# Scores in front of transposes, and odd heads' minima in front of the low half, in a four-layer attention kernel

## The reference

```python
def _L1_xattn_ref(text_hidden, vision_tokens, vision_mask, Wq, Wk, Wv, Wo):
    q = (text_hidden @ Wq).reshape(B, T_text, 16, 128).transpose(0, 2, 1, 3)
    k = (vision_tokens @ Wk).reshape(B, T_vis, 8, 128).transpose(0, 2, 1, 3)
    v = (vision_tokens @ Wv).reshape(B, T_vis, 8, 128).transpose(0, 2, 1, 3)
    k, v = jnp.repeat(k, 2, axis=1), jnp.repeat(v, 2, axis=1)
    scores = jnp.einsum('bhtd,bhsd->bhts', q, k) / scale
    attn = jax.nn.softmax(jnp.where(mask, scores, -jnp.inf), axis=-1)
    out = jnp.einsum('bhts,bhsd->bhtd', attn, v)
    return out.transpose(0, 2, 1, 3).reshape(B, T_text, 2048) @ Wo
...
x = x + _L0_xattn_ref(_layernorm(x), fside, ctx)
x = x + _L0_ffn_ref(_layernorm(x), w1, w2, w3)
x = x + _L1_xattn_ref(_layernorm(x), ctx, mask, Wq, Wk, Wv, Wo)
x = x + _L1_ffn_ref(_layernorm(x), router, sh_gate, sh_up, sh_down, r_gate, r_up, r_down)
```

## Time and profile before

| what | value |
|---|---|
| median of 3 runs | 386.31 us (386.14 to 386.44) |
| the profiled execution | 386.44 us, of which 384.7 us are the span from the first to the last instruction |
| TensorE matmuls | 373.3 us busy, 97% of the span |
| TensorE weight loads | 351.8 us, 91% |
| VectorE | 299.6 us, 78% |
| ScalarE | 233.9 us, 61% |
| GpSimd | 162.2 us, 42% |
| mean granted TensorE clock | 0.998 of full speed |

### The profile page before, as it was taken

How to read it: one execution, slowest core, us unless ns; L and a number is a source line. 1 busy time by engine, 2 the same in 40 slices (tenths; PEclk the granted TensorE clock), 3 DMA queues, 4 the chain that set the end, 5 groups by cost and what they waited for, 6 DMA issues and landing times.

```text
span 384.7 us, 8390 instructions
## 1 busy us (share of the span) xinstructions
PE 373.3 (97%) x2966; PEld 351.8 (91%) x2966; DVE 299.6 (78%) x982; ACT 233.9 (61%) x616; POOL 162.2 (42%) x260
## 2 busy tenths in 40 slices
PE   6899999999999999999999999999999999999996
PEld 6798789999798999999999999999999999999896
DVE  4798889889967889888767999887768876765644
ACT  1798787867544466766554466766554676664332
POOL 2113876874633344344453345246343333332232
PEclk9999999999999999999999999999999999999999
DMA  7999210000000200000000200000000000000000
GB/s 248 337 373 398 71 32 2 2 2 0 3 2 0 82 5 3 2 1 3 0 29 2 60 1 2 0 3 3 1 29 2 0 3 0 3 0 2 29 2 27
DMA packets 15193, 16.93 MB, mean 44 GB/s; under 512 B 1584, under 2 KB 14128, under 8 KB 15152
## 3 DMA queue, kind: packets, MB, share of 16 engines
q1 hardware_dynamic: 15152, 16.40, 12.7%
HBM read 15.34 MB, written 1.05 MB: 43 GB/s over the span
## 4 chain that ended last, share of the span: by engine, by line
PE 76%; DVE 12%; ACT 5%; POOL 3%; issue 2%; DMA 1%; DVEq 0%; SPq 0%; POOLq 0%
PE bank_qa L405 11%; PE bank_u L640 7%; PE bank_o L659 7%; PE bank_pt L624 7%; PE bank_s L604 6%; PE bank_s L405 5%; PE bank_o L663 4%; PE bank_u L644 3%; PE bank_s L612 3%; PE bank_s L522 3%; PE bank_pt L405 3%; PE bank_u L744 2%; PE bank_x L414 2%; PE bank_pt L522 1%; ACT prob L1010 1%
## 5 line engine op out<-in xcount | busy, mean ns | idle before, releaser
L1314 POOL TENSOR_SCALAR prob<-prob,row_inv,valid_b 128x256 f32<-128x256 f32 x128 | 70.3, 559 | 84.0 <-DVE row_inv L1684 84.0
L1010 ACT ACTIVATE prob<-prob,row_min 128x256 f32<-128x256 f32 x128 | 64.1, 503 | 40.9 <-DVE row_min L1676 40.8
L1689 DVE TENSOR_TENSOR pt_lo<-bank_pt,pt_hi 128x512 fp32r<-128x512 f32 x64 | 43.9, 686 | 14.8 <-ACT pt_hi L963 14.8
L1676 DVE CUSTOM_DVE_ANT_0 prob<-bank_s,masked 128x256 f32<-128x256 f32 x128 | 48.5, 417 | 0.9 <-ACT masked L992 0.6
L1325 POOL TENSOR_TENSOR act_lo<-act_raw,act_hi 128x256 fp32r<-128x256 f32 x32 | 24.1, 754 | 44.3 <-ACT act_hi L1077 44.2
L963 ACT ACTIVATE pt_hi<-bank_pt 128x512 fp32r<-128x512 f32 x64 | 37.6, 587 | 4.0 <-PE bank_pt L624 3.7
L624 PE MATMUL bank_pt<-ident,prob 128*128 128x128 f32 x256 | 39.5, 275 | 0.5 <-POOL prob L1314 0.3
L604 PE MATMUL bank_s<-cxT_hi,qa_hi 128*128 128x256 f32 x128 | 38.0, 319 | 0.0
L405 PE MATMUL bank_qa<-xt_hi,a_hi 128*128 128x256 f32 x126 | 35.0, 278 | 0.0
L405 PE MATMUL bank_qa<-xt_lo,a_hi 128*128 128x256 f32 x126 | 35.0, 278 | 0.0
L405 PE MATMUL bank_qa<-xt_hi,a_lo 128*128 128x256 f32 x126 | 35.0, 278 | 0.0
(11 more groups left out here) (325 smaller groups left out, 1190.2 us busy)
## 6 DMA issues: line engine op xcount, KB each, us to landing
wq_raw<-in_wqT SPq DMA_DIRECT2D x4, 512.0 KB, 8.7
wo_raw<-in_wo SPq DMA_DIRECT2D x4, 512.0 KB, 7.7
w_raw<-in_w12T SPq DMA_DIRECT2D x2, 704.0 KB, 7.1
gate_raw<-in_gateT SPq DMA_DIRECT2D x2, 576.0 KB, 7.3
up_raw<-in_upT SPq DMA_DIRECT2D x2, 576.0 KB, 9.0
down_raw<-in_downT SPq DMA_DIRECT2D x2, 576.0 KB, 10.8
x<-in_x SPq DMA_DIRECT2D x4, 256.0 KB, 5.9
guT<-in_guT SPq DMA_DIRECT2D x4, 256.0 KB, 3.6
```

What stands on the lines that cost most here:

```text
L1010: act.activation(row, row, ACT.Exp, scale=-1.0, bias=row_min[:, h % 2, t:t + 1], accum_out=row_sum[:, h % 2, t:t + 1]).then_inc(S["s_exp"], 1)
L1314: pool.tensor_scalar(row, row, row_inv[:, h % 2, t:t + 1], valid_b[:, 0:1], ALU.mult, ALU.mult).then_inc(S["s_norm"], 1)
L1676: dve.tensor_tensor_reduce(out=prob[:, h % 2, t, :], in0=src[:, t * T:(t + 1) * T], in1=masked[:, :], scale=1.0, scalar=3.0e38, op0=ALU.ad ...
L1689: dve.tensor_tensor(pt_lo[:, :, cols], bank["pt"][:, :].rearrange("p (s t) -> p s t", s=2), f32(pt_hi[:, :, cols]), ALU.subtract).then_inc ...
```

## The change

In TensorE's attention loop the scores of head h+2 are sent in front of the transposes of head h instead of behind them. In VectorE's loop the minima of head h+2 are taken in front of the low half of head h when h is odd, and behind it, as before, when h is even. Since the minima write over `prob` of head h, which the transposes read, the odd ones get a wait of their own for the transposes (`t_mm`); before, the low half's wait for `pt_hi` stood for that.

```diff
             def attention(b, beside=None):
 
                 for h in range(H):
-                    turn_probs(b, h)
                     if h + 2 < H:
                         scores(b, h + 2)
+                    turn_probs(b, h)
                     if h + 4 < H:
                         queries(b, h + 4)
...
                         row_inverses(b, h + 1)
                     if h >= 1 and h - 1 == mix_heads(mix_unit(h - 1))[-1]:
                         mix_lo(b, mix_unit(h - 1))
+                    if h % 2 == 1 and h + 2 < H:
+                        dve.wait_ge(S["t_mm"], H * b + h + 1)
+                        row_minima(b, h + 2)
                     probs_lo(b, h)
-                    if h + 2 < H:
+                    if h % 2 == 0 and h + 2 < H:
                         row_minima(b, h + 2)
```

## The result

The changed kernel takes **392.79 us** (392.68 to 392.95, 4 runs), the kernel before 386.23 us (386.06 to 386.44, 4 runs) beside it: a ratio of 1.0168, interval 1.0155 to 1.0180, or +6.6 us. The forecast was 391.0, in a range of 386.4 to 394.5. The profiled execution's span went from 384.7 to 391.1 us. All times here are medians; one execution of the kernel with the scores in front at odd heads took 740.11 us and is left out of its median.

What follows compares the result with a forecast made beforehand. TensorE was taken as the bound, without gaps inside the pairs. Losses at M's low-half waits summed to 4.9 us, less 0.2 for transposes: +4.7 on 386.44, 391.1, forecast as 391.0 us, range 386.4 to 394.5.

Steps and rivals of the forecast that it cites:

- TensorE sets the end and a new order can win only its few waits: Inside the 28 attention pairs: TensorE has no gaps; transposes wait at most 0.5 us in the run, 0.2 taken as gain.
- The tightest wait is M's for the low half: M's wait for the low half of a pair's second head has least slack: 0.36 to 1.19 us by place.
- The later transposes and the earlier minima add up at the odd low half: At the odd head's low half: 0.7 us from each, less VectorE's idle time there, 0.32 or nothing.
- first rival: Only one of the two delays counts, the later T being swallowed: about 386.7 us, no change; chance 0.08.
- second: Rival: minima fill VectorE's wait for `pt_hi`, so not slower: 385.9 us, or down to 384.2; chance 0.09.
- The undisturbed pair keeps 0.28: Batch 3, heads 6 and 7: odd low half 0.91 us late against 1.19 slack, no wait, 0.28 to spare.
- The rival with VectorE as the bound throughout: Four other pairs of batches 0 to 2 wait 0.4 us too, +4.8: 396 us; chance 0.08.
- The fourth pair loses 0.6: Heads 6 and 7, batches 0 to 2: low half 1.4 us late against 0.8, TensorE waits 0.6, three times.
- First and second pairs lose 1.1 and 0.9: First pairs: 0.4 us each in batches 1 and 2, 0.3 in batch 0; second pairs of batches 0 to 2: 0.3 each.
- The start of batch 3 loses 0.7: S(2) waits for `qa_lo`, delaying T(0); odd low half 1.24 us late against 0.53, 0.7 lost.
- The seventh pair loses 0.1, four times: Heads 12 and 13, each batch: low half about 0.8 us late against 0.8, 0 to 0.2 lost, 0.1 taken.
- the wait for `t_mm` costs nothing: Odd heads on VectorE: minima come after the inverses of head h+1, which end later than T(h), so no cost.

Runs made afterwards that it cites:

- the later transposes alone: Scores in front of transposes on TensorE, VectorE's order as in the kernel before: 392.48 us against 386.57, ratio 1.0151.
- the minima alone: VectorE's new order of minima only, TensorE's order as in the kernel before: 388.24 us against 386.57, ratio 1.0039.
- three heads, 0.6 us here: Kernel before with scores in front only at heads 1 and 3 of batch 0 and head 1 of batch 3: 385.93 us against 386.50, ratio 0.9985.

## Why the prediction was right, and what in it was off

- *TensorE sets the end and a new order can win only its few waits.* Right. The transposes' waits went (L624's idle time 0.5 to 0.0). The fifth pairs gained 0.24: in batch 1 two of T(8)'s transposes started 0.16 us behind the one ahead, while GpSimd finished, and now follow at 0.11. The third pairs gained 0.20, of which I know no cause.
- *The tightest wait is M's for the low half.* Not so, and the kernel before shows it. Its seventh pair in batch 1:

```profile
182.69 0.60 ACT L963 ACTIVATE pt_hi<-bank_pt 128x512 fp32r<-128x512 f32 x1 [0.56 <-PE bank_pt L624]
183.32 0.69 DVE L1689 TENSOR_TENSOR pt_lo<-bank_pt,pt_hi 128x512 fp32r<-128x512 f32 x1 [1.00 <-ACT pt_hi L963]
...
183.89 0.40 PE L640 MATMUL bank_u<-pt_hi,cx_hi 128*128 128x512 f32 x1
...
184.82 0.62 PE L644 MATMUL bank_u<-pt_lo,cx_hi 128*128 128x512 f32 x2
```

The low half ends at 184.01, 0.81 us ahead of L644; the high half ends at 183.29, only 0.60 ahead of L640. It is so in most pairs: 0.64 against 0.80 in the fourth, 0.32 against 0.53 at the start of batch 3, 0.05 against 0.36 in the first pairs of batches 1 and 2 (where the prediction saw it and still counted the low half). Only in the second pairs of batches 0 to 2 was the low half the tighter, by 0.04.

- *The later transposes and the earlier minima add up at the odd low half.* Right at the fourth pair, where either half alone costs 0.24 or 0.06 and both 0.76, and at the second (0.02 and 0.03 against 1.04 in all). Not true of the run as a whole: of +6.6 us the later transposes alone make +5.9, the minima alone +1.7, since without the minima in front other things are late. The first rival, under which the later T is swallowed and the time stays, is out by the +5.9; the second, under which VectorE hides it all, by the result.
- *The undisturbed pair keeps 0.28.* Measured 0.31, and no loss in the five middle pairs of batch 3. The rival with VectorE as the bound throughout is out: the third, fifth and sixth pairs of batches 0 to 2, which it had waiting, lose nothing.
- *The fourth pair loses 0.6.* It loses 0.76. The wait itself was 0.42 at the low half; the term lacked 0.11 us of restart behind each of two waits and the small wait of 0.05 at the high half, which makes 0.69.
- *First and second pairs lose 1.1 and 0.9.* Measured 1.33 and 1.04. The second pairs lose it at the low half. In the first pairs M is 0.73 late for the low half and 1.31 for the high half by the starts, and some of that is won back ahead of M.
- *The start of batch 3 loses 0.7.* Measured 1.06, and undoing that head brings 0.92 of it back. The rows:

```profile
308.65 0.68 DVE L1657 TENSOR_TENSOR qa_lo<-bank_qa,qa_hi 128x512 fp32r<-128x512 f32 x1
...
309.39 0.50 PE L612 MATMUL bank_s<-cxT_hi,qa_lo 128*128 128x256 f32 x2 [0.32 <-DVE qa_lo L1657]
...
311.74 0.66 PE L624 MATMUL bank_pt<-ident,prob 128*128 128x128 f32 x4
...
313.06 0.57 ACT L963 ACTIVATE pt_hi<-bank_pt 128x512 fp32r<-128x512 f32 x1
...
313.69 0.51 PE L640 MATMUL bank_u<-pt_hi,cx_hi 128*128 128x512 f32 x1 [0.59 <-ACT pt_hi L963]
```

S(2) waits for `qa_lo` as forecast, but the wait is handed on to the high half of head 1: M starts only when `pt_hi` ends at 313.63, while the low half behind it costs little more (0.16). The term looked at the low half alone.

- *The seventh pair loses 0.1, four times.* **This is the step that failed**: it loses 1.58 in all. I sized it by the low half, with a slack of 0.8; what is late is again M's high half, whose slack was 0.60. Batch 1, heads 12 and 13:

```profile
185.93 0.60 PE L624 MATMUL bank_pt<-ident,prob 128*128 128x128 f32 x4
...
186.56 0.60 ACT L963 ACTIVATE pt_hi<-bank_pt 128x512 fp32r<-128x512 f32 x1 [0.91 <-PE bank_pt L624]
...
186.83 0.40 PE L663 MATMUL bank_o<-c_hi,ut_lo 128*128 128x256 f32 x2
...
187.21 0.51 PE L640 MATMUL bank_u<-pt_hi,cx_hi 128*128 128x512 f32 x1
...
187.56 0.40 PE L640 MATMUL bank_u<-pt_hi,cx_lo 128*128 128x512 f32 x1
```

`pt_hi` follows its transposes at once and ends at 187.16, 1.23 us after they start. The two L663 matmuls stand 0.12 apart, so M would start at 187.06: with S in front, 1.13 us of matmuls are left between T(13) and M, where with S's 0.7 behind T(13) there were 1.83 and 0.60 to spare. M starts 0.15 late and its second matmul another 0.11, which makes 1.04 of the 1.58 over four batches. With the scores alone in front the seventh pairs lose no less (1.82), so it does not hang on the minima. That the wait for `t_mm` costs nothing was reasoned wrongly here too: T(13) ends after the inverses of head 14, and at each head 13 VectorE waits for it. It cost no time: the low half was still 0.16 us or more ahead of L644.

```profile
DVE prob L1676 <- PE bank_pt L624: 2.7, 4, 0.9
```

The losing terms came to 4.9 us and measured 7.3; the gains of the other places, 0.6, bring the sum to 6.7 (6.4 in the span, where the tail gives 0.3 back). The difference of 2.4 lies within the 2.8 that the prediction gave its 14 waits, but not wait by wait: the start of batch 3 and the seventh pairs missed by 0.3 to 0.4 each where 0.2 was allowed. So the mechanism, a fixed TensorE order that uses up the slack of M's waits, held, and at the second and fourth pairs it was the wait that was named. Elsewhere the right sign came with the wrong wait, and that the sum is not further off is in part luck: all 4.9 us were put at the low half, which cost 3.9 with its restarts, and the 3.7 at the high half were not in the sum.

Two readings of the prediction don't come out. The second rival's lower time should be 383.9 by its own terms (385.9 less 2), not 384.2. And of the 0.43 us that the load row left unfilled, only 0.18 stands before the 512-column matmuls' loads in that stretch (0.04 to 0.05 before each of four); 0.13 stands before transposes of the next batch and 0.12 inside T(8), where GpSimd was late. Of all this the change won the last, 0.1 us, and the row fell to 5.99 while the time grew. By the Trainium skill (Perfetto Trace Analysis, Identifying the Most-Contended Engine) TensorE's headroom is judged by that row, beside the share of peak arithmetic; in this kernel a small part of what it left was to be had, though it is the row on which waits are seen.

Left open: what the third pairs gained, a third of what the seventh pairs lost, and what M's low half would bring if it were sent later with VectorE's order changed to suit, which was not tried.

## What to carry to other kernels

Where an engine has no gap, moving a block of X us ahead of another takes X from the slack of *every* wait between the second block and its consumers. List them all with their slack, here the high half, the low half, the bank's release and the next query; the one that looks tightest need not be it. Each that breaks costs X less its slack, and a restart on top. A reordering that loses over the whole loop can still win at a few places, and may be kept there alone (three heads, 0.6 us here).

## What the runs showed of the hardware

In these traces a TensorE wait costs more than the wait. The second 512-column matmul after a stalled start comes 0.34 us after the first and not 0.23 (165.85 to 166.19, then on to 166.42 in the changed kernel), and two low matmuls take 0.74 us and not 0.62. That is 0.11 us each time, after the wait of some 0.05 us at the high half as after the one of 0.42 at the low half, so ten waits of 0.05 cost as much as one of 1.5. Behind a stalled transpose it was less (T(7) with scores in front at even heads: a row of 0.66 us and not 0.60).

The idle time that stands before a matmul row (0.27) and before its weight load (0.70) bracket the loss (0.53): the one is shortened by matmuls still running, the other begins while they run.
